# Layer norm ahead of the causal convolution: six of its eight row groups computed inside the second MLP's step loop

## What is computed

```python
h = _layernorm(x, axis=-1) * (1 + cb) + sb
x = x + gb * _L0_ffn_ref(h, ...)               # ends with the second gated MLP, its rows are y
...
h = _layernorm(x, axis=-1) * (1 + ca) + sa
x = x + ga * _L1_attn_ref(h, ...)
...
z = softmax(einsum('bse,he->bsh', h, W_A) * SCALING, axis=1)      # in _L1_attn_ref
v = einsum('bse,fe->bsf', h, W_V)
out = causal_convolution(z, v) @ W_O.T + b_O                      # in words: roll, tril, einsum
```

## Time and profile before

| | us |
|---|---|
| median of 3 runs | 1226.74 |
| lowest and highest | 1223.68, 1230.69 |
| the profiled execution's own time | 1231.43 |
| its span | 1229.6 |
| PE, DVE, ACT, POOL busy in it | 1075.1, 877.6, 818.4, 661.3 |

### The profile page before, as it was taken

The page is one execution under the profiler, slowest core; times in us unless marked ns, Lnnn a source line. Parts: engine busy times, 40 slices in busy tenths (PEclk is TensorE's granted clock), DMA queues, the critical chain, the costliest instruction groups (busy, mean ns, idle before and its releaser), DMA issues. The chain is left out here.

```text
span 1229.6 us, 33822 instructions
## 1 busy us (share of the span) xinstructions
PE 1075.1 (87%) x11683; PEld 741.5 (60%) x11683; DVE 877.6 (71%) x2948; ACT 818.4 (67%) x2658; POOL 661.3 (54%) x1070
## 2 busy tenths in 40 slices
PE   5799995699999997798999999988967788888987
PEld 3576673367777775465677777765644677743443
DVE  4689997588888886464888888875556212288788
ACT  3578884588889886234888898873338122378777
POOL 1578895788888885113888888871134200011122
PEclk9599997899999999999999999999989888989898
DMA  7000000112222111311121111120011676200000
GB/s 229 2 2 10 11 2 1 26 45 63 53 49 49 45 45 45 121 34 30 45 54 45 42 40 45 45 46 12 2 42 24 154 176 138 70 9 15 14 16 17
DMA packets 69566, 58.79 MB, mean 48 GB/s; under 512 B 42262, under 2 KB 53442, under 8 KB 69122
## 3 DMA queue, kind: packets, MB, share of 16 engines
q1 hardware_dynamic: 69411, 56.83, 18.9%
HBM read 29.40 MB, written 2.38 MB: 26 GB/s over the span
## 5 line engine op out<-in xcount | busy, mean ns | idle before, releaser
L1168 PE MATMUL psum<-wa_wqkv,wa_hT 128*128 128x512 f32 x384 | 188.5, 599 | 4.4 <-DVE wa_tmp L1032 3.2
L1124 ACT ACTIVATE wa_p<-psum,wa_nb 128x128 f32<-128x128 f32 x512 | 183.9, 399 | 4.3 <-DVE wa_nb L1048 4.2
L1048 DVE CUSTOM_DVE_ANT_0 psum<-psum,wa_bias 128x128 f32<-128x128 f32 x512 | 133.0, 322 | 51.4 <-PE psum L1197 51.4
L1014 POOL TENSOR_TENSOR wa_p<-wa_p,wa_rrs 128x512 f32<-128x512 f32 x128 | 133.2, 1041 | 47.5 <-DVE wa_rrs L1057 47.5
L1594 POOL TENSOR_TENSOR ex_total<-ex_total,mod 128x128 f32<-128x128 f32 x32 | 15.5, 483 | 234.2 <-DVE ex_total L1722 234.2
L1769 ACT ACTIVATE ex_yw<-psum,ex_w 128x128 f32<-128x128 f32 x384 | 107.0, 405 | 35.3 <-PE psum L1840 29.1
L1124 ACT ACTIVATION_READ_ACCUMULATOR wa_p<-psum,wa_nb 128x1 f32 x512 | 122.8, 240 | 0.0
L1840 PE MATMUL psum<-ex_wc,ex_hT 128*128 128x512 f32 x256 | 122.0, 633 | 0.0
L985 POOL TENSOR_TENSOR wa_qr<-wa_qr,wa_tmp 128x512 f32<-128x512 f32 x64 | 81.8, 1278 | 64.3 <-DVE wa_tmp L1032 64.3
L1134 ACT ACTIVATE wa_pT<-psum 128x512 f32<-128x512 f32 x128 | 76.5, 597 | 38.7 <-PE psum L1177 38.7
L1381 ACT ACTIVATE ml_gelu<-psum,ml_b 128x512 f32<-128x512 f32 (+1 forms) x48 | 32.9, 685 | 84.3 <-PE psum L1408 70.9
(11 more groups left out here) (256 smaller groups left out, 2985.5 us busy)
## 6 DMA issues: line engine op xcount, KB each, us to landing
wa_vm<-wa_v SPq DMA_DIRECT2D x127, 128.0 KB, 2.3
cv_toep<-cv_zpad SPq DMA_DIRECT2D x32, 256.0 KB, 4.4
cv_toep<-cv_zpad SPq DMA_DIRECT2D x16, 512.0 KB, 7.0
wa_tabs<-in_rotations_dram SPq DMA_DIRECT2D x2, 2048.0 KB, 8.1
wa_rows<-y_rows SPq DMA_DIRECT2D x31, 128.0 KB
wa_rows<-y_rows SPq DMA_DIRECT2D x31, 127.0 KB
x_rows<-in_L_attn_x_dram SPq DMA_DIRECT2D x4, 512.0 KB, 5.7
out_dram<-x_rows SPq DMA_DIRECT2D x32, 64.0 KB, 1.5
```

The lines of the kernel that those rows point to most:

```text
L1014: nc.gpsimd.tensor_tensor(p, p, cols_bc(rrs[:, t % 2, r, :], P), ALU.mult)\
L1048: m = nc.vector.tensor_tensor_reduce(out=s, in0=s, in1=edges, scale=-1.0, scalar=MAX_FLOAT, op0=ALU.add, op1=ALU.min, accum_out=nb[:, t % ...
L1124: e = nc.scalar.activation(pr[:, t % 2, r, h, :], sim_bank[r][:, P * h:P * h + P], ACT.Exp, bias=nb[:, t % 2, r, h:h + 1], scale=-1.0, acc ...
L1168: nc.tensor.matmul(bank, hT[:, t % 3, :], wqkv[:, INNER * k:INNER * k + INNER], start=True, stop=True).then_inc(done.sem, 1)
```

## The change

Residual, layer norm and normalised tiles of the convolution's groups 0 to 5 move from the second block into the second MLP's phases: `gated` on POOL at lag 4, `statistics` and `offsets` on DVE at lag 5, `inverse_std` on POOL at lag 5 ahead of the MLP's own, `normalized` on ACT at lag 5. Groups 6 and 7 stay at the second block's start. The normalised tiles overwrite y instead of going to a ring. The convolution's weights are loaded by SP during the MLP; PE turns them and ACT copies them at step 11, and ACT's table for exponentials is loaded at step 10. In the second block DVE does its weights and mixing ahead of the maxima, and the first exponential comes one iteration earlier. The statistics now signal once for four tiles.

```diff
+class ConvolutionRows:
+    IN_MLP = TILES // 4 - 2
+    def __init__(self, c, y, ctx):
+        sb = c.sb(ctx)
+        self.c, self.y = c, y
+        self.w_in = sb("cv_w_in", [P, 3, E])
+        self.waT, self.wvT, self.woT = sb("cv_waT", [P, CH]), sb("cv_wvT", [P, E]), sb("cv_woT", [P, E])
+        self.bo = sb("cv_bo", [P, E])
+        self.st6, self.mv = sb("cv_st6", [P, 4, 6]), sb("cv_mv", [P, TILES, 2])
+        self.rstd, self.shift = sb("cv_rstd", [P, TILES]), sb("cv_shift", [P, TILES])
+        sem = lambda name: c.sem(ctx, "cv_" + name)
+        def in_turn(name, n):
+            s = sem(name)
+            return [Signal(s, k, n) for k in range(n)]
+        self.loaded, self.p_w, self.a_w = sem("loaded"), sem("p_w"), sem("a_w")
+        self.g_gated, self.g_rstd = Signal(sem("g_gated")), Signal(sem("g_rstd"))
+        self.v_x, self.v_st, self.v_mv, self.v_eps = in_turn("v_x_stat", 4)
+        self.v_shift, self.a_norm = Signal(sem("v_shift")), Signal(sem("a_norm"))
...
+    def load(self, sp):
+        inp = self.c.inp
+        sp.dma_start(self.w_in[:, 0, :], inp["L1_attn_W_V"]).then_inc(self.loaded, 16)
+        sp.dma_start(self.w_in[:, 1, :], inp["L1_attn_W_O"]).then_inc(self.loaded, 16)
+        sp.dma_start(self.w_in[0:CH, 2, :], inp["L1_attn_W_A"]).then_inc(self.loaded, 16)
+        sp.dma_start(self.bo[:, :], inp["L1_attn_b_O"].unsqueeze(0).broadcast_to([P, E])).then_inc(self.loaded, 16)
+    def turn_weights(self, pe, bank):
+        nc, ident = self.c.nc, self.c.ident
+        pe.wait_ge(self.loaded, 64)
+        nc.tensor.transpose(bank[:, 0:P], self.w_in[:, 0, :], ident[:, :])
+        nc.tensor.transpose(bank[:, P:2 * P], self.w_in[:, 1, :], ident[:, :])
+        nc.tensor.transpose(bank[:, 2 * P:2 * P + CH], self.w_in[0:CH, 2, :], ident[0:CH, 0:CH]).then_inc(self.p_w, 1)
+    def copy_weights(self, act, bank):
+        nc = self.c.nc
+        act.wait_ge(self.p_w, 1)
+        nc.scalar.activation(self.wvT[:, :], bank[:, 0:P], ACT.Copy).then_inc(self.a_w, 1)
+        nc.scalar.activation(self.woT[:, :], bank[:, P:2 * P], ACT.Copy).then_inc(self.a_w, 1)
+        nc.scalar.activation(self.waT[:, :], bank[:, 2 * P:2 * P + CH], ACT.Copy).then_inc(self.a_w, 1)
+    def gated(self, gp, g):
+        c, t = self.c, self.tiles(self.y, g)
+        b = 4 * g // NT
+        c.nc.gpsimd.tensor_tensor(t, t, rows_bc(c.mod[:, 0, b, GB, :], 4), ALU.mult).then_inc(self.g_gated.sem, 1)
+    def inverse_std(self, gp, g):
+        self.v_eps.wait(gp, g)
+        t = slice(4 * g, 4 * g + 4)
+        self.c.nc.gpsimd.tensor_tensor(self.rstd[:, t], self.mv[:, t, 1], self.c.minus_half[:, 0:4], ALU.pow)\
+            .then_inc(self.g_rstd.sem, 1)
+    def statistics(self, dve, g):
+        nc, x = self.c.nc, self.c.x
+        self.g_gated.wait(dve, g)
+        t = self.tiles(x, g)
+        nc.vector.tensor_tensor(t, t, self.tiles(self.y, g), ALU.add).then_inc(self.v_x.sem, 1)
+        self.v_x.wait(dve, g)
+        for i in range(4):
+            m = nc.vector.bn_stats(self.st6[:, i, :], x[:, 4 * g + i, :])
+        m.then_inc(self.v_st.sem, 1)
+        self.v_st.wait(dve, g)
+        for i in range(4):
+            m = nc.vector.bn_aggr(self.mv[:, 4 * g + i, :], self.st6[:, i, :])
+        m.then_inc(self.v_mv.sem, 1)
+        self.v_mv.wait(dve, g)
+        var = self.mv[:, 4 * g:4 * g + 4, 1]
+        nc.vector.tensor_scalar(var, var, LN_EPS, None, ALU.add).then_inc(self.v_eps.sem, 1)
+    def offsets(self, dve, g):
+        self.g_rstd.wait(dve, g)
+        t = slice(4 * g, 4 * g + 4)
+        self.c.nc.vector.scalar_tensor_tensor(out=self.shift[:, t], in0=self.mv[:, t, 0], scalar=-1.0,
+                                              in1=self.rstd[:, t], op0=ALU.mult, op1=ALU.mult)\
+            .then_inc(self.v_shift.sem, 1)
+    def normalized(self, act, g):
+        self.v_shift.wait(act, g)
+        for t in range(4 * g, 4 * g + 4):
+            m = self.c.nc.scalar.activation(self.y[:, t, :], self.c.x[:, t, :], ACT.Identity,
+                                            scale=self.rstd[:, t:t + 1], bias=self.shift[:, t:t + 1])
+        m.then_inc(self.a_norm.sem, 1)
...
+        def conv_rows(eng, do, lag):
+            def f(g):
+                if g - first < conv.IN_MLP:
+                    do(eng, g - first)
+            return [] if more else [(f, lag)]
...
+            else:
+                conv.load(sp)
...
+            def conv_gated(g):
+                v_y.wait(gp, g)
+                if g - first < conv.IN_MLP:
+                    conv.gated(gp, g - first)
+            return Phase(conv_rows(gp, conv.inverse_std, 5) + [(inverse_std, 0)] +
+                         ([] if more else [(conv_gated, 4)]), first, GROUPS)
...
-            return Phase([(residual, 4), (statistics, 0), (multiply, 2), (normalize, 0)], first, GROUPS,
+            return Phase([(residual, 4)] + conv_rows(dve, conv.statistics, 5) +
+                         [(statistics, 0), (multiply, 2), (normalize, 0)] + conv_rows(dve, conv.offsets, 5), first, GROUPS,
...
-            return Phase([(gelu, 2), (hn_columns, 1)], first, GROUPS,
-                         between={2: lambda: nc.scalar.preload_act_table_set("gelu_and_others")},
+            between = {2: lambda: nc.scalar.preload_act_table_set("gelu_and_others")}
+            if not more:
+                between[10] = lambda: nc.scalar.preload_act_table_set("natural_log_exp_and_others")
+                between[11] = lambda: conv.copy_weights(act, turn_bank)
+            return Phase([(gelu, 2), (hn_columns, 1)] + conv_rows(act, conv.normalized, 5), first, GROUPS,
+                         between=between,
...
+            def conv_weights():
+                a_hn.wait(pe, last)
+                conv.turn_weights(pe, turn_bank)
+            return Phase([(up, 2), (turn, 1), (down, 3)], first, GROUPS, begin=lambda: wait_layer(pe, l),
+                         between=None if more else {11: conv_weights})
...
+                late = range(conv.IN_MLP, GROUPS)
+                for g in late:
+                    conv.gated(gp, g)
+                for g in late:
+                    conv.inverse_std(gp, g)
                 on_gpsimd.fill(gp)
                 gp.wait_ge(v_w, 2)
                 for g in range(GROUPS):
-                    gp.wait_ge(a_norm, GT * g + GT)
+                    conv.a_norm.wait(gp, g)
...
                 dve.sem_inc(v_conv, 1)
-                for g in range(GROUPS + 4):
-                    if g < GROUPS:
-                        statistics(g)
-                    if 1 <= g <= GROUPS:
-                        offsets(g - 1)
-                    if g >= 4:
-                        group_max(g - 4)
-                    if g == PER_B + 4:
-                        probabilities(0)
+                late = range(conv.IN_MLP, GROUPS)
+                for g in late:
+                    conv.statistics(dve, g)
+                for g in late:
+                    conv.offsets(dve, g)
                 weights()
                 on_vector.mixing(dve)
+                for g in range(GROUPS):
+                    group_max(g)
+                    if g == PER_B:
+                        probabilities(0)
                 probabilities(1)
...
-                    pe.wait_ge(a_norm, GT * g + GT)
+                    conv.a_norm.wait(pe, g)
                     if g >= 2:
                         pe.wait_ge(a_h, g - 1)
-                    else:
-                        pe.wait_ge(a_w, 3)
                     for k in range(GT):
-                        m = nc.tensor.transpose(turn_bank[g % 2][:, P * k:P * k + P], rows[:, g % 2, k, :],
+                        m = nc.tensor.transpose(turn_bank[g % 2][:, P * k:P * k + P], y[:, GT * g + k, :],
                                                 c.ident[:, :])
...
-                pe.wait_ge(loaded, 48)
-                nc.tensor.transpose(z_bank[:, 0:P], w_in[:, 0, :], c.ident[:, :])
-                nc.tensor.transpose(z_bank[:, P:2 * P], w_in[:, 1, :], c.ident[:, :])
-                nc.tensor.transpose(z_bank[:, 2 * P:2 * P + CH], w_in[0:CH, 2, :], c.ident[0:CH, 0:CH])\
-                  .then_inc(p_w, 1)
...
-                nc.scalar.preload_act_table_set("natural_log_exp_and_others")
-                act.wait_ge(p_w, 1)
-                nc.scalar.activation(wvT[:, :], z_bank[:, 0:P], ACT.Copy).then_inc(a_w, 1)
-                nc.scalar.activation(woT[:, :], z_bank[:, P:2 * P], ACT.Copy).then_inc(a_w, 1)
-                nc.scalar.activation(waT[:, :], z_bank[:, 2 * P:2 * P + CH], ACT.Copy).then_inc(a_w, 1)
-                for g in range(GROUPS + 2):
-                    if g < GROUPS:
-                        normalized(g)
+                for g in range(1, GROUPS + 2):
+                    if g in (2, 3):
+                        conv.normalized(act, conv.IN_MLP + g - 2)
                     if 1 <= g <= GROUPS:
                         h_columns(g - 1)
                     if g >= 2:
                         outputs(g - 2)
```

(52 more changed lines are left out.)

43 lines of the change are left out of this document (9 added, 34 removed).

## The result

The changed kernel took 1219.8 us (median of 7 runs, 1217.0 to 1222.6) against 1227.3 of the kernel before (7 runs, 1223.7 to 1233.5). The ratio is 0.9928, with a 95% interval of 0.9900 to 0.9956, which is 8.8 us less (5.4 to 12.3). The ratio is taken over all executions; the two medians alone are 7.5 us apart. Forecast were 1218.4 and 8.3 us less. The profiled execution has a span of 1218.0 us (1229.6 before).

A forecast was written before the change was run, and what follows sets the result against it. PE bounds the second MLP; behind it a chain hopping between engines sets the pace. MLP body 0, tail +1.9 and fourth weight round −10.15 give −8.3 us, from median 1226.74 to 1218.4 us; range 1213 to 1225.

The forecast's parts named there:

- The MLP's body at zero: Second MLP: six groups' added work fits beside PE, DVE ending before its next due residual; cost 0, upper end 2.7 us.
- the first rival: MLP: DVE and POOL block each other at every meeting, PE waits 2.7 us; total gain 5.6, 1221.1 us; chance 0.18.
- The tail, +1.9: MLP's end: group 5's late offset, ACT's four tiles and three weight copies start the block 1.9 us later (1.5 to 3).
- part 3: Second block's start: ACT waits for group 6's offset, then low clock; last v copied at +30.95 against +39.19, 8.2 us less.
- the sign that the prediction gives at its end: Block start to convolution: some 42 to 43 us instead of 54.0 in the new profile.
- The order of DVE's work: Second block: DVE's weights and mixing ahead of its maxima, over long before the softmax scaling, which takes 1.27 instead of 2.06 us.
- The term that was mis-sized: Weight rounds: from PE's fourth round to the convolution the old 8.63 us stay.
- The third rival: Before the fourth round: shorter PE gaps, clock perhaps not low, project(2) perhaps earlier; up to 3 to 4 us more; chance 0.11.
- The second rival: Block's columns: PE's clock stays low, 4.84 instead of 2.63 us per group; 4.1 us slower, 1230.8; chance 0.10.
- The fourth: Rival at the convolution's start: it hangs on the toeplitz loads, so nothing moves; chance 0.03.

The follow-up runs named there:

- The last run: Changed kernel with tiles of groups 6 and 7 two iterations later, group 5's in next block, weight rounds filled with identity transposes: 1209.7 us, ratio 0.9859.
- 16 fillings: Changed kernel plus 16 identity transposes on PE between its third turn and second projection, results unchanged: 1215.4 us, ratio 0.9873.
- the tiles later: Changed kernel with ACT's normalised tiles of groups 6 and 7 two loop iterations later in its queue: 1213.5 us, ratio 0.9867.
- 28 fillings: Changed kernel plus 28 identity transposes on PE between its third turn and second projection: 1213.5 us, ratio 0.9878.

## Why the prediction was right

*The MLP's body at zero.* The period stayed 8.27 us, and the whole MLP up to D 58.6 us. DVE ended a full step at S+7.8 (expected S+8.15): normalize began at S+6.1 and not behind the gating, but was slowed by it from 1.11 to 1.65. The Trainium skill (SBUF — State Buffer, "Who interferes with whom") states, for a DVE instruction in a mode that uses both of its ports (it lists `tensor_scalar`, which normalize is), that whichever of DVE and GpSimd issues second fully blocks for the other's whole instruction. The rows agree in direction, since normalize began 0.78 us before the gating's end (884.87 against 885.65) and took 0.54 longer, though not the full 0.78. In which mode it ran and which of its four instructions waited, the merged row does not show. The step's cover was measured: with 2.4 us more of DVE per step PE waited 2.7 us in all, beyond a lateness of about 4 us, which is the tolerance that the first rival was worked out from. The rival itself did not occur; DVE's adds met no POOL work, and of the three meetings that it priced only the one at normalize came, at 0.54.

*The tail, +1.9.* Measured +1.7 (from D to the block: 3.9 before, 5.6 after). That ACT's four tiles held the block is shown by taking them out: 1.2 us back. The copies stayed in that run, and what the other 0.5 is made of was not tested.

*The block's start.* The steps of part 3 stand beside the trace (block start 909.78) like this: ACT's late tiles at +6.9, measured +6.9; second projection +9.75, measured +9.9; third +14.6, measured +14.6; seventh +26.1, measured +26.4; last v copied +30.95, measured +31.2; fourth round +35.2, measured +35.4. The wait that the change adds was priced by removing it together with the low clock behind it (5.3 us), and that low clock by keeping the clock up (2.1 us, which are part of the 5.3; the prediction's 3.73 + 1.11 against 2.63 says 2.2). Two steps ahead of it were off and cost nothing, since ACT waited for the offset all the same: group 0 was projected at +5.0, not +3.8, at the low clock, and PE then idled 4.1 us, not 6. And the sign that the prediction gives at its end, 42 to 43 us from block start to convolution, does not follow from its own terms, which give 35.2 + 8.63 = 43.8; measured were 44.8.

*The order of DVE's work.* 2.0 expected when undone, 1.9 measured at the fourth round.

*The term that was mis-sized.* From the fourth round to the convolution I took over the 8.63 us of the row. It measured 9.44, and that is most of why the stretch gained 7.5 us and not 8.3. The clock was low in the rounds of both kernels; what differs is when. Before, it was at 0.50 from 954 on and full again within 960 to 962, about half way through the eight large products:

```profile
958.09 5.21 PE L1800 MATMUL psum<-ex_wT,ex_mix 128*128 128x512 f32 x8
```

```profile
960.00:962.00 2.00, 2.00 (x5) 0.65 (x3) 0.57 (x1) 0.60 (x1) 0.68 (x1) 0.80 0.06 14
```

After, it fell within a microsecond of the fourth round's start (0.50 from 946, the turn itself still 0.66 us instead of 1.11) and stayed low until 952 to 953, through four fifths of the products' time, and they took 6.26 us instead of 5.21. The third rival had expected the shorter gaps of PE to leave the clock full there; it fell all the same, in every kernel whose rounds were not filled (8.1 to 9.9 us). The last run shows what full clock gives: 6.7.

*The second rival*, low clock through all the columns, did not occur: it was full again from 927 on, as before the change. *The fourth*, the toeplitz loads, did not either: the convolution's start names ACT as its releaser in every trace, down to the 39.1 us of the last run.

The whole time moved by 8.8 us with an interval of 5.4 to 12.3, and the stretch by 7.5; the 1.3 between them is inside what executions of one code differ by, and I don't give it a cause. For the 16 fillings the same comparison leaves more: 9.0 us less by the stretch (48.9 against 57.9) and 15.6 by the ratio, with 11.5 as the lower end. One trace is one execution, and the clock's state in the rounds differs between them. The mean granted clock of the whole kernel was 0.955 to 0.959 in the six executions with 16 fillings and 0.942 to 0.954 in the seven of the changed kernel, so the time may have been gained elsewhere too; whether that is all of it stays open.

## What to carry to other kernels

Work moved under a bound engine is free only as far as the queues of the others still end before their next due instruction; count the queue of one full step, and then look at the last step, where nothing covers it: here the moved groups were free but for the last one, which cost 1.7 us. When a loop is shortened, look which instruction now stands at the head of an in-order queue for work that nobody needs yet: two groups of tiles placed two iterations too early cost 5.3 us with the low clock behind the wait, more than half of what the whole move brought.

## What the runs showed of the hardware

With the same instructions, the stretch from the convolution's first matmul to the end took between 257.8 us (in the run with DVE's old order) and 266.1 us (with the tiles later). Its last 161 to 169 us went with the granted clock: 160.8 to 164.2 us at a mean of 0.95, 165.5 to 169.1 at 0.91, in ten traces. These are its lines in the run with DVE's old order and in the one with the tiles later:

```profile
1058.74:1219.50 160.76, 137.71 (x461) 66.69 (x456) 134.09 (x370) 120.08 (x435) 30.41 (x64) 0.95 0.05 14
```

```profile
1050.93:1220.00 169.07, 146.23 (x502) 72.00 (x496) 134.38 (x371) 122.14 (x438) 30.39 (x64) 0.91 0.05 13
```

So a difference of a few microseconds between two traces has to be read from a stretch, not from the spans. And a clock once full did not stay so: in the run with 16 fillings PE was idle from 920.5, and the clock was still full at 921 to 923 and low when work came at 923.45, while with 28 fillings and an idle time of 1.05 us it held. The same idle time of 2.35 us, ahead of the block, left it full in some traces and low in others.
